# Five of ten shared units inside the routed experts, five behind them and partly in the final pass, with deeper buffers of rows

## What is computed

```python
# T = 4096 tokens, E = 32 experts, K = 4 of them a token, C = 160 slots an expert
Xp = x[slots_token].reshape(E, C, d)
G = jnp.einsum('ecd,edi->eci', Xp, W_gate)
U = jnp.einsum('ecd,edi->eci', Xp, W_up)
Y = jnp.einsum('eci,eid->ecd', jax.nn.silu(G) * U, W_down)
Yf = Y.reshape(EC, d) * slots_w[:, None]
out = jnp.zeros((T, d), x.dtype).at[slots_token].add(Yf)
shared = jax.nn.silu(x @ shared_gate.T) * (x @ shared_up.T) @ shared_down.T
return (out + shared).reshape(b, s, d)
...
x = _layernorm(x + _L1_ffn_ref(x, ...), axis=-1)
```

## Time and profile before

| | us |
|---|---|
| median of three runs | 1964.71 |
| the three runs | 1964.71, 1968.96, 1964.3 |
| profiled execution, its own time | 1963.74 |
| its span | 1961.8 |

### The profile page before, as it was taken

The page is one execution under the profiler, slowest core; times in us unless marked ns, Lnnn a source line. Parts: engine busy times, 40 slices in busy tenths (PEclk is TensorE's granted clock), DMA queues, the critical chain, the costliest instruction groups (busy, mean ns, idle before and its releaser), DMA issues. The chain is left out here.

```text
span 1961.8 us, 35601 instructions
## 1 busy us (share of the span) xinstructions
PE 1833.9 (93%) x12032; PEld 1643.8 (84%) x12032; DVE 1483.0 (76%) x4074; ACT 1039.5 (53%) x2694; POOL 836.0 (43%) x863
## 2 busy tenths in 40 slices
PE   7999999999999999999999999999999999978880
PEld 6788888888888887888789999999999999977870
DVE  7978787787878796656677888888888888863436
ACT  5434343333333333333477777777777777735653
POOL 1232323232323220000244566666666666754776
PEclk9999999999999999999999999999999999988995
DMA  3201010000101003473200010000000000127867
GB/s 121 95 1 33 1 33 23 12 22 12 33 1 50 30 22 120 139 264 127 93 12 18 21 41 26 22 21 20 19 19 20 19 19 14 40 75 186 198 141 260
DMA packets 102003, 118.81 MB, mean 61 GB/s; under 512 B 12567, under 2 KB 93723, under 8 KB 101184
## 3 DMA queue, kind: packets, MB, share of 16 engines
q1 hardware_dynamic: 89104, 108.42, 17.0%
q0 software_dynamic: 12288, 8.11, 2.7%
q10 hardware_dynamic: 432, 0.02, 0.0%
HBM read 75.50 MB, written 57.10 MB: 68 GB/s over the span
## 5 line engine op out<-in xcount | busy, mean ns | idle before, releaser
L282 POOL TENSOR_TENSOR kept_q_rows<-kept_q_rows 128x512 f32<-128x512 f32 x128 | 203.5, 1590 | 527.3 <-DVE kept_q_rows L547 527.3
L1716 POOL TENSOR_TENSOR kept_raw<-kept_raw,mla_row_inv 128x512 f32<-128x512 f32 x192 | 199.2, 1038 | 258.4 <-DVE mla_row_inv L2056 257.2
L372 ACT ACTIVATE kept_q_rows<-rwkv_r 128x512 f32<-128x512 f32 x128 | 76.6, 599 | 399.3 <-DVE rwkv_o_low L468 396.7
L1874 ACT ACTIVATE kept_raw<-kept_raw,mla_least 128x256 f32<-128x256 f32 (+1 forms) x512 | 227.7, 446 | 74.2 <-DVE mla_least L2040 71.7
L2040 DVE CUSTOM_DVE_ANT_0 kept_raw<-mla_score,kept_mask 128x256 f32<-128x256 f32 (+1 forms) x512 | 157.1, 352 | 82.7 <-PE mla_score L2412 52.5
L532 DVE TENSOR_TENSOR kept_q_rows<-rwkv_v,kept_q_rows 128x512 f32<-128x512 f32 x128 | 88.1, 688 | 113.2 <-PE rwkv_v L583 110.9
L539 DVE TENSOR_TENSOR_SCAN rwkv_state<-rwkv_decay_w,kept_q_rows 128x256 f32<-128x256 f32 x256 | 166.0, 691 | 4.1
L1799 POOL DMA_INDIRECT slots<-mla_x_out,mla_slot_now x128 | 130.6, 1020 | 30.8 <-issue 23.2
L1890 ACT ACTIVATE mla_p_high<-mla_turn 128x512 fp32r<-128x512 f32 x192 | 114.0, 594 | 48.1 <-PE mla_turn L2420 46.5
L2050 DVE TENSOR_TENSOR mla_p_low<-mla_turn,mla_p_high 128x512 fp32r<-128x512 f32 x192 | 128.1, 667 | 2.1 <-ACT mla_p_high L1890 2.1
L2420 PE MATMUL mla_turn<-kept_ident,kept_raw 128*128 128x128 f32 x768 | 116.1, 274 | 8.5 <-DVE mla_p_low L2050 8.5
(11 more groups left out here) (505 smaller groups left out, 6265.6 us busy)
## 6 DMA issues: line engine op xcount, KB each, us to landing
kept_raw<-in_experts SPq DMA_DIRECT2D x27, 384.0 KB
kept_raw<-in_rkvo SPq DMA_DIRECT2D x16, 512.0 KB
moe_y_in<-sums SPq DMA_DIRECT2D x32, 256.0 KB, 4.7
sums<-ffn_empty SPq DMA_DIRECT2D x12, 512.0 KB
slots<-ffn_empty SPq DMA_DIRECT2D x16, 361.2 KB
moe_e_rows<-slots SPq DMA_DIRECT2D x31, 180.6 KB
kept_x_in<-x SPq DMA_DIRECT2D x18, 256.0 KB, 17.0
mla_x_res<-x SPq DMA_DIRECT2D x17, 256.0 KB
```

The costliest lines, as they stand in the source:

```text
L282: nc.gpsimd.tensor_tensor(gate[:, c % 2, :], key[:, c % 2, :], gate[:, c % 2, :], ALU.mult).then_inc(gated_done, 1)
L1716: nc.gpsimd.tensor_tensor(unit, unit, row_inv[:, v % PR, 0:len(heads)].rearrange("p (h a) -> p h a", a=1) .to_broadcast([P, len(heads), ke ...
L1874: last = nc.scalar.activation(probs[:, v % PR, i * keys:(i + 1) * keys], masked[:, v % 2, i * keys:(i + 1) * keys], ACT.Exp, bias=least[:, ...
```

## The change

- `SRING` = 12 buffers of gathered rows instead of 8; results and their semaphores keep a ring of 8. SyncE asks at step e for the slots of expert e+9 (`SRING - SLACK`), which wait for the landing of expert e-3. Slots 8 is loaded ahead of the loop.
- `PACE` = 6: a unit's pieces fall on every second step of six, `PIECES`, and begin at expert 1. `INSIDE` = 5 units go into the loop.
- `XROWS` = 6 buffers of unit rows instead of 4; unit u+4 is asked for at unit u's first piece.
- Five units are behind the loop. VectorE does its steps for three of them (`BEFORE`) ahead of the final pass and the others' after positions 0, 2 and 4.

```diff
 RING = 8
+SRING = 12
+SLACK = 3
...
-PACE = 4
+PACE = 6
+PIECES = {0: 0, 2: 1, 4: 2}
+XAHEAD = 4
+XROWS = 6
...
-INSIDE = 7
+INSIDE = 5
+BEFORE = 3
...
         def unit_of(e):
 
-            return e // PACE, e % PACE
+            if e == 0:
+                return 0, None
+            return (e - 1) // PACE, PIECES.get((e - 1) % PACE)
...
             def load_slots(e):
-                if e >= RING:
-                    sp.wait_ge(e_turned, e - RING + 1)
+                if e >= SRING:
+                    sp.wait_ge(e_turned, e - SRING + 1)
                     for a in range(2):
-                        sp.wait_ge(y_added[e % RING][a], 16 * (e // RING))
+                        sp.wait_ge(y_added[(e - SRING) % RING][a], 16 * ((e - SRING) // RING + 1))
...
             load_x(3)
+            load_slots(8)
 
             for e in range(E):
                 u, piece = unit_of(e)
-                if piece == 0 and u >= 1 and u - 1 + XRING < LATE:
-                    load_x(u - 1 + XRING)
+                if piece == 0 and u + XAHEAD < LATE:
+                    load_x(u + XAHEAD)
                 if e + WRAW < E:
                     load_w(e + WRAW)
-                if e >= 1 and e - 1 + RING < E:
-                    load_slots(e - 1 + RING)
+                if 8 <= e + SRING - SLACK < E:
+                    load_slots(e + SRING - SLACK)
...
-            for u in range(INSIDE, LATE):
+            for u in range(INSIDE, INSIDE + BEFORE):
                 if u > INSIDE:
                     add_shared(u - 1)
-                if u + 1 < LATE:
-                    x_low(u + 1)
-                    shared_hidden(u)
-                    shared_low(u)
+                x_low(u + 1)
+                shared_hidden(u)
+                shared_low(u)
...
                     combine(g, p)
-                    if p == 0:
-                        shared_hidden(LATE - 1)
-                        shared_low(LATE - 1)
-                    if p == 1:
-                        add_shared(LATE - 1)
+                    u = INSIDE + BEFORE + p // 2
+                    if p % 2 == 0 and u <= LATE:
+                        add_shared(u - 1)
+                    if p % 2 == 0 and u < LATE:
+                        if u + 1 < LATE:
+                            x_low(u + 1)
+                        shared_hidden(u)
+                        shared_low(u)
```

More of the change, by code:

```diff
@@ L2599, in moe_phase @@
         ws_part = kept_weights(wq_high)
-        x_rows = s.sb("x_rows", [P, XRING, UT, D])
+        x_rows = s.sb("x_rows", [P, XROWS, UT, D])
         xt_part = both("xt", [P, 2, KD, UNIT])
@@ L2606, in moe_phase @@
         wd_part = both("wd", [P, WRING, D])
-        e_rows = s.sb("e_rows", [CH2, RING, 2, ROW])
+        e_rows = s.sb("e_rows", [CH2, SRING, 2, ROW])
         e_cols = s.sb("e_cols", [P, 2, KD, CAP])
@@ L2631, in moe_phase @@
         consts_set = s.sem("consts_set")
-        rows_in = [s.sem(f"rows_in{r}") for r in range(XRING)]
+        rows_in = [s.sem(f"rows_in{r}") for r in range(XROWS)]
         transposed = s.sem("transposed")
@@ L2646, in moe_phase @@
         w_low = s.sem("w_low_done")
-        slots_in = [s.sem(f"slots_in{r}") for r in range(RING)]
+        slots_in = [s.sem(f"slots_in{r}") for r in range(SRING)]
         e_turned = s.sem("e_turned")
@@ L2675, in slot_rows @@
         def slot_rows(e):
-            return first_slots[:, :, :] if e == 0 else e_rows[:, e % RING, :, :]
+            return first_slots[:, :, :] if e == 0 else e_rows[:, e % SRING, :, :]
         def wait_slots(eng, e):
             if e > 0:
-                eng.wait_ge(slots_in[e % RING], 16 * (e // RING + (0 if e % RING == 0 else 1)))
+                eng.wait_ge(slots_in[e % SRING], 16 * (e // SRING + (0 if e % SRING == 0 else 1)))
         def unit_of(e):
-            return e // PACE, e % PACE
+            if e == 0:
+                return 0, None
+            return (e - 1) // PACE, PIECES.get((e - 1) % PACE)
         def unit_rows(dram, u):
@@ L2698, in load_x @@
             def load_x(u):
-                if u >= XRING:
-                    sp.wait_ge(total_done, u - XRING + 1)
-                sp.dma_start(x_rows[:, u % XRING, :, :], unit_rows(x3, EARLY + u)).then_inc(rows_in[u % XRING], 16)
+                if u >= XROWS:
+                    sp.wait_ge(total_done, u - XROWS + 1)
+                sp.dma_start(x_rows[:, u % XROWS, :, :], unit_rows(x3, EARLY + u)).then_inc(rows_in[u % XROWS], 16)
             def load_w(e):
@@ L2709, in load_slots @@
             def load_slots(e):
-                if e >= RING:
-                    sp.wait_ge(e_turned, e - RING + 1)
+                if e >= SRING:
+                    sp.wait_ge(e_turned, e - SRING + 1)
                     for a in range(2):
-                        sp.wait_ge(y_added[e % RING][a], 16 * (e // RING))
+                        sp.wait_ge(y_added[(e - SRING) % RING][a], 16 * ((e - SRING) // RING + 1))
                 sp.dma_start(slot_rows(e),
                              slots_dram[e * CAP:(e + 1) * CAP, :].rearrange("(a p) d -> p a d", p=CH2))\
-                    .then_inc(slots_in[e % RING], 16)
+                    .then_inc(slots_in[e % SRING], 16)
             load_slots(1)
@@ L2881, in _ @@
                     x_high(u + 1)
-                busy = piece < 2 and u < INSIDE
+                busy = piece in (0, 1) and u < INSIDE
                 if e + 2 < E:
@@ L2941, in add_shared @@
                 dve.wait_ge(shared_done, u + 1)
-                dve.wait_ge(rows_in[u % XRING], 16 * (u // XRING + 1))
+                dve.wait_ge(rows_in[u % XROWS], 16 * (u // XROWS + 1))
                 nc.vector.tensor_tensor(tiles(EARLY + u), down_ps[:, :].rearrange("p (t d) -> p t d", d=D),
-                                        x_rows[:, u % XRING, :, :], ALU.add).then_inc(total_done, 1)
+                                        x_rows[:, u % XROWS, :, :], ALU.add).then_inc(total_done, 1)
             def weights_low(e):
@@ L3047, in turn_x @@
             def turn_x(u):
-                pe.wait_ge(rows_in[u % XRING], 16 * (u // XRING + 1))
+                pe.wait_ge(rows_in[u % XROWS], 16 * (u // XROWS + 1))
                 if u >= 1:
@@ L3053, in turn_x @@
                         last = nc.tensor.transpose(xt_ps[:, k * UNIT + j * P:k * UNIT + (j + 1) * P],
-                                                   x_rows[:, u % XRING, j, k * P:(k + 1) * P], ident[:, :])
+                                                   x_rows[:, u % XROWS, j, k * P:(k + 1) * P], ident[:, :])
                 last.then_inc(transposed, 1)
```

## The result

| | us |
|---|---|
| median after, 20 runs | 1968.3 (1963.62 to 1971.12) |
| median before, 20 runs beside them | 1964.76 (1960.21 to 1968.96) |
| ratio after to before, 95% | 1.0018 [1.0012, 1.0024] |
| profiled execution after, its own time | 1969.72, span 1967.7 |

What follows compares the result with a forecast made beforehand. Scatter landings were taken to bound the loop's first part and VectorE the final pass. Scatter end -2.2 and pass +4.3 sum to +2.1 us on the median 1964.71, giving 1966.8 us, range 1955 to 1976.

Steps and rivals of the forecast that it cites:

- The pass, +4.3: Final pass: VectorE's added steps behind positions 0, 2 and 4 lengthen it by 4.3 us, bounds +3.1 and +6.
- the 1.2 us wait for unit 9's up product: Final pass behind position 3: VectorE waits 1.2 us for TensorE, its products priced at the lower clock.
- The port rule, given 0.05: Rival, final pass: two VectorE low parts block against GpSimd's additions, +2.2 us on top, 1969.0; chance 0.05.
- Landings pace the scatters: Loop: after expert 1 GpSimd waits for scatter landings, never TensorE or ACT; 14 us lost ahead of expert 24.
- the 7.4 to 8.3 named: Loop sign: forecast wrong if the mean cycle of two experts leaves 7.4 to 8.3 us.
- Landings of 3.3 to 6.4 us: Loop: a scatter's landing takes 3.3 us without loads in flight, up to 6.4 with them.
- The start, -1.2: First experts: expert 3 up to 1.6 us earlier, less the fuller first burst; -1.2 us, bounds 0 to -1.6.
- Twelve buffers, -0.6: Loop's tail: last slots asked for at expert 19's landing, not 23's, so expert 24's 0.6 us wait goes.
- Scatter end, -2.2: End of scatters: start -1.2, twelve buffers -0.6 and six unit buffers -0.4 sum to -2.2 us; bounds -14.3 and +6.
- The rivals' -14 and +6: Scatter end: landings never late, -14.3 us (rival's chance 0.18); all as slow as the worst, +6 (0.20).
- Five units behind, cost 0: Between loop and pass: TensorE finishes by 1904, thirteen us ahead of the first addition; cost 0.
- The pass hides its steps (0.07): Rival, final pass: GpSimd sets the pace, VectorE's steps fall in gaps; only -2.2 stays, 1962.5; chance 0.07.

Runs made afterwards that it cites:

- b_mixed: Kernel before with only the changed placing of VectorE's steps for the units behind the loop (some behind positions 0, 2 and 4): ratio 1.0021.
- b_pace_mixed: Changed kernel with eight buffers of gathered rows instead of twelve, fifth unit load waiting for expert 7's step: ratio 1.0008 to the kernel before.
- a_third: Changed kernel, from expert 7 on loading only output weights, a third of each expert's weight bytes (no longer computes the layer): ratio 0.9976 to the kernel before.
- b_front: Kernel before with the last unit's three VectorE steps also put ahead of the final pass, loop unchanged: ratio 1.0000.
- a_front: Changed kernel with all VectorE steps for the units behind the loop put ahead of the final pass: ratio 0.9998 to the kernel before, median 1963.34 us.
- b_pace_tail: Kernel before with one unit in six, five inside, six unit buffers, all VectorE steps but the last unit's three ahead of the pass: ratio 1.0027.
- b_pace: Kernel before with one unit in six, five inside, six unit buffers, all VectorE steps ahead of the pass: ratio 1.0028.

## Why the prediction was right, point by point

- **Direction and size.** +2.1 was forecast and +3.5 measured. It was a sum of two terms of opposite signs. The pass carried the direction and is shown by experiment; the gain ahead of it, -2.2, came out as +0.5 in the profile. That the sum still came near is partly luck: the pass was priced 1 us too high, which made up for some of the gain that wasn't there.
- **The pass, +4.3.** It is the change's loss: 35.3 to 38.65 us in the profile (+3.3), 38.8 with the placing alone, 33.5 without. The terms inside were sized less well. Position 1 was to lose 0.2 and lost 1.0, since the low part of unit 8 took 1.73 us; position 3 was to lose 3.7 and lost 3.1, since the 1.2 us wait for unit 9's up product didn't come: VectorE was later, and TensorE had its full clock again for that product (granted 0.96 from 1930.10 to 1932.00), where I had priced three at the lower one. That wait was one of the signs I had named, and by it the account of the pass was wrong in this place. Behind position 3 came 0.25 instead of 0.6.
- **The port rule, given 0.05.** It bit once, not twice: 1.73 us at 1925.60 (1.79 in b_mixed), 0.69 for unit 9's low part at 1933.68. The first started beside GpSimd's addition of 1925.50 to 1926.78 and ended 0.55 us behind it, the second started when GpSimd had ended the one of 1931.91 and was idle. As the Trainium skill has it (SBUF — State Buffer, SBUF: two separate sides), the pair is held for a whole instruction, and the row agrees with +1.04 us. In all three kernels with the new placing and all weights it hit the same step (1.75 us in b_pace_mixed), so it should have been a term of the sum and not a rival.
- **Landings pace the scatters.** This held: a_third. A wait put down to ACT was again a landing: SyncE dates that of expert 0 at 1798.86, and expert 2 (1799.64, 2.39 us "ACT") started 0.78 us later, as in before. The cycle of two experts between 4 and 20 was 7.9 us, inside the 7.4 to 8.3 named.
- **Landings of 3.3 to 6.4 us.** The worst was misread: the trace before already had one of 7.4, expert 0's (1789.30 to 1796.71), in the first burst. And the 3.3 of 1884.28 to 1887.55 was not without loads: SyncE issued three from 1885.81 on, inside it. The size is right for a landing alone all the same: from the last scatter to SyncE's first load of sums it is 3.26 us before (1912.55 to 1915.81) and 3.23 after (1914.84 to 1918.07).
- **The start, -1.2.** The gain came, 2.05 us at expert 1 and 1.0 at expert 3, and was lost at expert 4 (+1.9). I had let the burst's 2.7 us lie "just under experts 1 to 3" with 6.05 as the landing that it causes; it was 7.9. At expert 4 my own bound of 0 was already too good. At expert 12 the changed kernel was 1.4 us ahead again, which one profile doesn't tell from chance.
- **Twelve buffers, -0.6.** This is the step that failed. "The trigger and the bytes stay" leaves out that SyncE's releases are in bursts where its order catches up: at the start and on expert 19's landing, where the two last unit loads followed as well. Expert 23's wait of 2.50 us stands there in place of the 0.6 us that were to go, and at the end eight experts ran at 3.4 us, not the ten to twelve named. The two runs of the buffers alone stand at +4 us by the ratios. In them the full rate does begin some two experts earlier; its worth isn't seen.
- **Scatter end, -2.2.** It was +0.5 in the profile. But one profile doesn't settle 2 us here: the unchanged loop ended at 133.1, 131.1 and 132.7 in before, b_front and b_mixed, the changed one at 133.6 and 132.0 in after and a_front. The rivals' -14 and +6 are excluded.
- **Five units behind, cost 0.** This was right, with TensorE done 11 us ahead of the first addition. "With the loop's end of before still about in time" was right as well for three units ahead: in b_pace_mixed the first addition came 6.9 us behind the last scatter, before 6.6. It doesn't hold for more: 8.8 with four ahead (b_pace_tail) and 16.5 with five (b_pace).
- **The pass hides its steps (0.07)** is refuted by a_front and b_mixed.

Put together by the ratios: the placing costs 4 us (b_mixed), pace and unit buffers give some 2.5 (b_pace_mixed 1.0008 against b_mixed 1.0021, its interval holds 0), the four buffers more cost about 2 (1.0018 against 1.0008, holds 0 as well). Only the first of these is shown. Alone, in the old loop, the four buffers cost 4 us in two runs, so the three numbers needn't add up in another order.

## What to carry to other kernels

A step that is moved behind the arrival of data that everybody waits for costs its length, less what other waits there would have cost anyway, though the engine idled 14 us just ahead of it: the steps behind position 0 took 4.2 us and moved position 1 by 2.3 (5.6 instead of 3.3 in a_front). Fill the wait first. Deeper buffers in front of a chain that is paced by the landing of another queue's transfers didn't speed it up here; they bought distance for the engine that fills them, and their loads came in bursts where the issuing engine's order catches up. Before counting a buffer as free, ask what is issued back to back when its wait has long been met.

## What the runs showed of the hardware

- The landing of an indirect, adding transfer of 80 rows of 1 KB depended on what else was in flight: 3.2 to 3.3 us alone (the last scatter, before and after), 3.2 to 6.5 among one or two experts' loads (after, experts 4 to 19; before, 3.2 to 6.4 for experts 1 to 23), and 7.1 to 7.9 in the first burst, with the DMA engines at 1.00 and 1.04 (after, experts 0 to 3). I had held it near 6.4 by the rule of turns between queues (the Trainium skill, DMA: Bandwidth & Descriptors, Queues, rings and completion order); that it rose further with the burst isn't what I read from it.
- A VectorE operation with two SBUF operands beside a GpSimd addition took 1.73 to 1.79 us instead of 0.69, in three kernels at the same step (unit 8's low part in after, b_mixed and b_pace_mixed).
- TensorE's granted clock, at 0.50 after 13.7 us of idling, was back at full (0.96 as the mean of its stretch) in the third of three products of twelve matmuls, 5.8 us after the first had started. For unit 9's output, at 1934.43 behind 2.7 us of idling, it was at 0.50 again.
- Profiled executions of one loop differed by up to 2 us in where the last scatter lies (before, b_front, b_mixed) and by 4.2 in b_pace, b_pace_tail and b_pace_mixed; differences below that came out only by the timed ratios.
